# Norm of the next sample in buffers of its own, four projections in two other banks, and a new order of calls

## What is computed

```python
h = _layernorm(x) * (1 + ca) + sa
x = x + ga * attention(h)            # q, k: norm per head; causal softmax; Wu
h = _layernorm(x) * (1 + cb) + sb
x = x + gb * ffn(h)                  # silu(w1 h) * (w2 h), gelu(h1 .), gelu(h2 .), w3
# layer 1, with its own modulation
x = x + ga * selective_scan(h)       # h = (1 + A dt) h + B dt x over time; y = C h
x = x + gb * linear(quantise(h))
```

## Time and profile before

| | |
|---|---|
| median of 3 runs | 4414.48 us (4412.8 to 4420.98) |
| the profiled execution | 4410.43 us, span 4408.7 us |
| mean granted TensorE clock | 0.919 |
| PE busy | 3700.5 us (84% of the span) |
| DVE busy | 3558.4 us (81%) |
| POOL busy | 2530.8 us (57%) |
| ACT busy | 2435.4 us (55%) |

### The profile page before, as it was taken

One profiled execution on the slowest core, in us unless ns is written; L12 is line 12 of the kernel. 1 busy time (PEld: TensorE's weight loads), 2 busy tenths in 40 slices (PEclk: granted clock), 3 DMA queues, 4 the chain that ended last, 5 costly groups with the idle time before them and its releaser, 6 DMA issues. The chain is left out here.

```text
span 4408.7 us, 51342 instructions
## 1 busy us (share of the span) xinstructions
PE 3700.5 (84%) x17261; PEld 2188.9 (50%) x17261; DVE 3558.4 (81%) x3917; ACT 2435.4 (55%) x3413; POOL 2530.8 (57%) x1895
## 2 busy tenths in 40 slices
PE   5688888989899898989888898989989898998623
PEld 3364544636464554636464463646455463646301
DVE  4514788979898887989888897989889898988795
ACT  2344555647565565646555564656556564655532
POOL 0131756648484755758474674848475574847462
PEclk8697999999999999999999999999999999999856
DMA  4630211203030110203020120303011020302000
GB/s 176 228 106 1 78 34 39 77 6 111 1 101 15 63 53 25 92 6 111 1 90 27 38 78 6 111 1 101 15 63 53 26 90 6 111 1 87 15 5 5
DMA packets 69436, 247.79 MB, mean 56 GB/s; under 512 B 9600, under 2 KB 10112, under 8 KB 68736
## 3 DMA queue, kind: packets, MB, share of 16 engines
q1 hardware_dynamic: 66816, 235.28, 16.1%
q10 hardware_dynamic: 2304, 8.39, 0.5%
HBM read 212.19 MB, written 31.46 MB: 55 GB/s over the span
## 5 line engine op out<-in xcount | busy, mean ns | idle before, releaser
L668 POOL TENSOR_TENSOR kept<-kept,hb 128x512 f32<-128x512 f32 x640 | 809.5, 1300 | 28.2 <-DVE hb L1821 28.2
L1812 DVE TENSOR_TENSOR_SCAN hb<-ps,hb 128x512 f32<-128x512 f32 x640 | 741.8, 1203 | 6.5 <-ACT ps L1332 5.6
L636 POOL TENSOR_TENSOR kept<-kept,hb 128x1024 f32<-128x1024 f32 x128 | 334.8, 2632 | 698.1 <-DVE hb L1756 639.1
L881 PE MATMUL ps<-hid_bhi,wring 128*128 128x512 f32 x1536 | 623.2, 406 | 17.3 <-issue 13.8
L881 PE MATMUL ps<-hid_blo,wring 128*128 128x512 f32 x1536 | 608.0, 396 | 0.0
L1332 ACT ACTIVATE ps<-kept,a_neg 128x512 f32<-128x512 f32 x640 | 431.7, 691 | 263.3 <-DVE hb L1812 263.3
L621 POOL TENSOR_SCALAR_AFFINE_SELECT room<-room 128x512 f32<-128x512 f32 x256 | 237.8, 945 | 570.8 <-ACT room L1498 570.8
L1882 DVE TENSOR_REDUCE room<-ps 128x4 f32<-128x2048 f32 (+3 forms) x256 | 375.6, 1488 | 234.1 <-PE ps L1060 232.8
L881 PE MATMUL ps<-hid_ahi,wring 128*128 128x512 f32 x1280 | 514.4, 402 | 18.7 <-POOL hid_alo L683 17.9
L881 PE MATMUL ps<-hid_alo,wring 128*128 128x512 f32 x1280 | 503.5, 393 | 0.0
L1498 ACT ACTIVATE room<-ps 128x2048 f32<-128x2048 f32 (+1 forms) x192 | 305.3, 1590 | 256.7 <-PE ps L1086 256.1
(11 more groups left out here) (188 smaller groups left out, 7580.5 us busy)
## 6 DMA issues: line engine op xcount, KB each, us to landing
wring<-w_hi SPq DMA_DIRECT2D x352, 512.0 KB, 3.3
kept<-in_wffn SPq DMA_DIRECT2D x22, 512.0 KB, 6.0
w_hi<-wring SPq DMA_DIRECT2D x22, 512.0 KB, 6.9
w_lo<-wrest SPq DMA_DIRECT2D x22, 512.0 KB, 3.9
xn<-in_x_fm SPq DMA_DIRECT2D x17, 512.0 KB, 3.5
out_fm<-xc ACTq DMA_DIRECT2D x16, 512.0 KB, 5.1
room<-in_wmod SPq DMA_DIRECT2D x2, 1536.0 KB, 8.2
win<-in_win SPq DMA_DIRECT2D x1, 1024.0 KB, 8.4
```

What stands on the lines that cost most here:

```text
L636: pool.tensor_tensor(pair_of(acc, h), pair_of(acc, h), pair_of(hb, h), ALU.add).then_inc(tail_acc, 2)
L668: pool.tensor_tensor(acc[:, m, :], acc[:, m, :], hb[:, s % 8, :], ALU.add).then_inc(acc_done, 1)
L881: mm = pe.matmul(bank(bk), wring[:, r % 3, at + k * P:at + (k + 1) * P], src[i][:, k, :], start=(k == 0 and i == 0), stop=(k == K - 1 and ...
L1812: dve.tensor_tensor_scan(hb[:, s % 8, :], bank(2 + m % 2), hb[:, s % 8, :], 0.0, ALU.mult, ALU.add).then_inc(scanned, 1)
```

## The change

- **Norm of the next sample.** It gets semaphores of its own (`next_*`), its square goes to `qk_sq`, its logarithm to `next_log`, and its affine step (`next_affine`) is run in the same pass, in place in `ln_x`, with a modulation that DVE's new `pick_next` copies into `m_next`. `att_norm` is gone; `project` and `project_v` read `ln_x`. A pass without other parts does this once ahead of sample 0. The table load in `next_rstd` now stands behind the wait for the variance.
- **Scalings** take their factor from PSUM: the exponential is written to the bank of the variance instead of `ln_s[:, 1, :]`.
- **Projections** use banks 6 and 7 in turn instead of 0 to 3, and `head_var` bank 4 alone; each of the four has its own `qk_rs`. So projections 2 and 3 wait for `normalise` 0 and 1, and `pre_mean`, `pre_var` and `project_v` wait too.
- **Scores** of quads 0 and 2 wait for the even versions, of quads 1 and 3 for the odd, and only for the two of their half. `even_version` is a call apart from `normalise`.
- `gate_in(1)` waits for the scaling instead of the logarithm.
- **The four lists** are written in another order almost throughout.

The core of the diff, without the lists:

```diff
-            act.activation(ln_s[:, 1, :], ln_s[:, 0, :], ACT.Exp, scale=-0.5).then_inc(ln_rstd, 1)
+            act.activation(bank(bk), ln_s[:, 0, :], ACT.Exp, scale=-0.5).then_inc(ln_rstd, 1)
...
-            dve.tensor_tensor(ln_x[:, :, :], ln_x[:, :, :], bcast_c(ln_s[:, 1, :]), ALU.mult).then_inc(ln_norm, 1)
+            dve.tensor_tensor(ln_x[:, :, :], ln_x[:, :, :], bcast_c(bank(bk)), ALU.mult).then_inc(ln_norm, 1)
...
-        VAR_BANK = (2, 3, 0, 1)
+        QK_BANK = (6, 7, 6, 7)
...
             def project(i):
                 if att:
-                    pe.wait_ge(att_in, since(att_in, DC))
                     if i == 0:
-                        pe.wait_ge(b_ready, since(b_ready, 0))
-                        pe.wait_ge(b_copied, since(b_copied, 0))
-                    elif i == 1:
-                        pe.wait_ge(y_ready, since(y_ready, 0))
-                    else:
-                        pe.wait_ge(scanned, since(scanned, 0))
-                        pe.wait_ge(qk_logged, since(qk_logged, i - 1))
+                        pe.wait_ge(att_in, since(att_in, 0))
+                    if i >= 2:
+                        pe.wait_ge(qk_normed, since(qk_normed, i - 1))
...
+                if u == 0:
+                    pe.wait_ge((ver_even, ver_odd)[p], since((ver_even, ver_odd)[p], 2 * c + 2))
                 if quad == 0:
-                    if u == 0:
-                        pe.wait_ge(ver_even, since(ver_even, 4))
-                        pe.wait_ge(ver_odd, since(ver_odd, 4))
...
-                    pe.wait_ge((ln_cent, ln_log)[m], k_pre.number)
+                    pe.wait_ge((ln_cent, ln_norm)[m], k_pre.number)
...
+            def next_affine():
+                if nxt:
+                    act.wait_ge(next_norm, since(next_norm, 1))
+                    act.wait_ge(next_mod, since(next_mod, 1))
                     for c in range(DC):
+                        act.activation(ln_x[:, c, :], ln_x[:, c, :], ACT.Identity, bias=m_next[:, SA + c:SA + c + 1],
+                                       scale=m_next[:, CA + c:CA + c + 1]).then_inc(att_in, 1)
...
             def next_rstd():
+                if nxt:
+                    act.wait_ge(next_var_done, since(next_var_done, 1))
+                    if fin:
+                        act.wait_ge(quantised, since(quantised, 2 * QN))
+                    if ffn:
+                        act.preload_act_table_set(LN_EXP)
+                    act.activation(next_log, bank(7), ACT.Ln, bias=eps[:, 0:1]).then_inc(next_ln, 1)
+                    act.wait_ge(next_ln, since(next_ln, 1))
+                    act.activation(bank(7), next_log, ACT.Exp, scale=-0.5).then_inc(next_rstd_ready, 1)
...
             def pre_centre():
                 if pre:
                     if att:
-                        dve.wait_ge(att_in, since(att_in, DC))
+                        dve.wait_ge(v_done, since(v_done, 2))
+                        dve.wait_ge(qk_done, since(qk_done, 4))
```

726 lines of the change are left out of this document (380 added, 346 removed).

## The result

The changed kernel takes 4291.97 us (median of 4 runs, 4288.44 to 4298.70), the kernel before 4413.64 us in the same comparison (4407.22 to 4420.98). The ratio is 0.9726, with a 95% interval of 0.9706 to 0.9746: 121.7 us less. The forecast was 59 us less, so the sign is right, the size is half of what came, and the time lies 6 us under the range. The profiled execution took 4293.9 us, with a span of 4292.2.

What follows compares the result with a forecast made beforehand. No engine alone bounds a pass; attention's chain and two handovers do, with three full engines in the last 105.5 us. +0.4 - 3.2 - 1.3 = -4.1 us per pass, times 14, plus two opening passes: 4355 us, range 4298 to 4430.

Steps and rivals of the forecast that it cites:

- the walk: New lists timed instruction by instruction with the old trace's durations, every matmul at 2.4 GHz, no slip between queues.
- term 2: Chain of attention: att_proj(3) ends 5.2 us earlier in the walk, 2.0 us taken off, so -3.2 us per pass.
- term 3: From attention to the up-projections: PE gains 2.1 us, DVE 0.6; the middle, -1.3 us per pass, was entered.
- the two passes ahead of the loop: Claimed to give perhaps 1 us each.
- term 1: Start of a pass: norm moved into the pass before, tail_in 0.8 us later than in this boundary; +0.4 us per pass.
- The opening: The two passes ahead of the loop, claimed to gain perhaps 1 us each.
- the end: The last two passes, which have no attention, claimed to hardly change.
- the load costs nothing: Start of a pass: the 1.28 us table load behind the variance wait is free, as DVE works without a gap.
- slower: Rival: lead never won back after scores(3,0) behind out_proj(0); +2.2 us per pass, 4445 us; chance 0.17.
- Much faster: Rival: denser PE removes the stretches at 1.2 GHz, another 5 us per pass, 4285 us; chance 0.22.
- The factor in PSUM: Scalings: 1.22 us with the factor in PSUM; were it 2.54, term 1 would be 1.3 us higher.

Runs made afterwards that it cites:

- e11: Changed kernel with the table load in next_rstd ahead of its wait for the variance and next_scale ahead of times_c(11, 1) on DVE: 4277.7 us.
- e13: e12 with up(0) ahead of spread(0, 3) on PE: 4287.4 us.
- e12: e11 with ffn_centre ahead of head_scan(1, 1) and ffn_scale ahead of times_b(2, 0) on DVE: 4277.7 us.
- e7: Changed kernel with the second quantisation, fin_back(1) and fin_ff(0) behind attention's end again, as in the kernel before: 4390.9 us.
- e1: Changed kernel with its early start of the scores taken back: scores(0, 0) behind project_v(0) and pre_mean, maxima behind normalise(3): 4389.9 us.
- e9: Changed kernel up to the third unit of quad 0, from there the call order of the kernel before on all four engines: 4668.3 us.
- e3: Changed kernel's functions, buffers and banks with the call order of the kernel before, moved only where the new banks force it: 4696.2 us.
- e8: Changed kernel with scores(3, 0) and find_max(3, 0) ahead of out_proj(0), clip_dt, weigh(0) and out_add(0); out_proj(1) behind the turned scores: 4355.0 us.
- e4: Changed kernel with the factor of each norm written to SBUF again, so scalings read both operands from SBUF: 4298.0 us.
- e5: Kernel before with the changed kernel's order around quad 3, head_spread(0, 1) kept right behind values(2, 2): 4425.3 us.
- e14: e11 with up(0) ahead of spread(0, 3) on PE and the norm in its old place: 4293.8 us.

## Why the prediction was right in sign and too small

- **The step that failed:** the allowances taken off the walk, 2.0 us in term 2 and the halving of term 3, and the two passes ahead of the loop, priced at 1 us each. By the means of the fourteen passes term 2 is -4.8 us where I entered -3.2, term 3 is -2.4 for -1.3, and term 1 is -0.3 for +0.4. That is 3.4 us a pass too little, 48 us in all: 22, 15 and 10. The opening gave 17.6 us more than I entered, and the end took back 8.3.
- **The pass as the unit, and the chain of attention as its bound:** right. Fourteen passes bring 105 of the 116.5 us, nearly all of it ahead of the first product. A pass has 244.1 us where I named 246 to 247.
- **Term 1 (start of the pass, +0.4):** nearly right. From the first product to the next tail_in the mean pass has 98.8 us after and 99.2 before. The scaling of 1.22 us came out. So did the sentence that the load costs nothing in this order: DVE was ready at 1529.42 for a factor of 1529.32, behind its times_c. What it left out is that the load and next_scale() moved together get PE's wait back, 1.2 us (e11). The Trainium skill's "ScalarE: Activation LUTs" (what a table load costs) adds a drain of about 1.38 us to a load; no run here shows it: the next ACTIVATE starts 0.01 us behind the load (1527.99 in after), and in e13's rows a load stands between two ACTIVATEs with no more than 0.02 us on either side.
- **Term 2 (attention, -3.2):** the walk was good, the deduction was not. Milestones of the pass from 1292.13, forecast and measured: scores(0,0) end 9.4 and 10.8; maxima (1,2) 46.0 and 49.5; scores(3,0) 80.5 and 84.0; turned scores (2,0) 87.0 and 90.0; turned scores (3,0) 107.3 and 109.8; att_proj(3) 127.8 and 128.3. The walk ran 3 us ahead in the middle and was right again at the end. scores(3,0) came 3.5 us later than before, not level, and turned scores (2,0) 4.9 later, so the first half of the rival "slower" came true more strongly than I had it; the walk's other half, that quad 3 gets it back, held. The walk gave -5.2, and I entered -3.2 by taking 2.0 us off for matmuls at 1.2 GHz and for slip. That deduction is the larger part of what failed. The slips are there, but the kernel before has its own: in the mean att_proj(3) ends at 129.1, 1.3 us behind the walk, and before at 133.9, 0.9 behind the pass that I walked beside. The two nearly cancel, and 0.4 us was the right allowance.
- **Term 3 (hand-over, -1.3):** the walk said 16.2 us from att_proj(3) to the first product and the trace has 16.2. The gain is 2.2 to 2.3. I had halved it towards DVE's 0.6, since DVE is full afterwards; that was the second failing step, 1 us a pass. The walk's reason holds too: the product waits last for the second split (16.1), as walked (16.0). What the walk did not have is that spread(0, 3) stands there 0.4 us ahead of it, so that a faster norm alone brings nothing (e12). That fin_ff and the quantisation went ahead of attention's end was right. With it went 6.5 of the 7.8 us at 1.2 GHz; e7, which undoes it, loses 8.7 us a pass, its own wait included.
- **The opening (about -2):** wrong by 17.6 us. The two passes ahead of the loop's steady ones have attention too, and there the early start pays more than the 8 us of its lead; e1, whose opening is 585.6, has none of it. I had priced these passes as if only the boundary were in them.
- **The end (hardly changes):** it takes 8.3 us more. e9, which has only the first part of the new lists, takes 310.8 us for it, e3, with the old lists in the same buffers, 302.3. So it comes from the new order of the pass's first part, run in passes that have no attention. The first of the two last passes has 6.4 of the 8.3 us (203.6 against 197.2). There DVE centres the norm of pre at 12.7 us into the pass in after and e9, behind tail_out(0, ...) and pick_mod(), and at 6.7 before and in e3. That this is the wait that counts was not shown by undoing it.
- **The rivals.** "Slower" blamed out_proj(0) ahead of scores(3, 0); e8 turned the two and lost 63 us, but with a wait of its own, so it does not show that the place is the best one. "Much faster" named 4285, and 4292 came, but hardly by its mechanism: it had the 25 us at 1.2 GHz go, and 18.6 of 22.0 are still there, 12.7 of 13.5 in attention. Only in the hand-over did they go. A number can come true for another reason.
- **The factor in PSUM:** I gave it 1.3 us at the boundary and some tenths elsewhere. In e4 the scaling at the boundary is 0.8 us longer and the others are not; the kernel's time moves by less than can be told.

The summary by single undoings: without the early start 98 us are lost, without the end order 105, without the early quantisation 99, all of a gain of 122. Each loss sits mainly in another part of the pass (quad 0, quad 3, the hand-over), and each holds some clock or a wait of its own. Of the three, the end order and the early start were also tried without the rest, and neither helped (e5, e9). They are one arrangement, and their prices do not add up to the gain.

## What to carry to other kernels

When you have walked a new order instruction by instruction against a trace that already contains its slow stretches and waits, enter what the walk gives; an allowance charged to the new side alone cost this forecast 1.6 us a pass, 22 us of 57. Undo one part of a new order to price it, and read in the trace where the loss falls, since a hand-made reordering brings waits of its own (six times here: DVE for a spread, PE for POOL's sums, gates for a norm, PE for a late quantisation, an addition for a projection, ACT's table load for a spread). When a product comes earlier and the time stays, read the queue of the engine that takes it before you blame the clock. A lead that seems to vanish beside the old order may only have been spent on other work, and the undoing shows it at full value.

## What the hardware showed that I had not expected

The same instructions on the same engines gave passes of 242.4 and of 246.1 us in one execution. The slower has 20.5 us at 1.2 GHz in its attention, the other 10.2, and ends attention 3.5 us later (131.7 against 128.2). Stretches of after, 115 to 125 us into the two passes, the first at 2.4 GHz, the second at both levels:

```profile
1407.00:1417.00 10.00, 9.57 (x70) 5.39 (x71) 9.63 (x16) 2.85 (x4) 4.67 (x7) 1.00 0.01 2
```

```profile
1893.00:1903.00 10.00, 8.99 (x54) 4.33 (x54) 7.92 (x14) 3.84 (x5) 4.38 (x6) 0.66 0.01 2
```

And passes of 242.3 to 242.5 us return in after, e11, e12, e13 and e14, though their starts, norms and first products differ by up to 2.4 us: e11's gain over after is mostly that more of its passes have this length (eleven of its fourteen passes are under 243 us, six of after's). So a difference of a few us in one pass of one trace says little here; the mean over the fourteen does.
